# Second scan of a two-layer SSM/MoE kernel: who empties the bank of a gate projection

## The reference

```python
proj = hidden_states @ in_proj_w.T
gate = proj[..., :D_IN]                       # D_IN = 512
xBC  = proj[..., D_IN:D_IN + CONV_DIM]        # CONV_DIM = 768
...
xBC = silu(conv_b + causal_conv(xBC, 4 taps))
y   = _ssd(x * dt[..., None], dt * A, Bm, Cm) + D * x
hg  = y * silu(gate)
y   = hg * rsqrt(mean(hg * hg) + EPS) * norm_w
return y @ out_proj_w.T
```

## Time and profile before

| what | us |
|---|---|
| median of 3 runs (lowest to highest) | 1231.43 (1230.41 to 1232.26) |
| the profiled execution | 1236.41 |
| its span, first to last instruction | 1234.7 |
| PE busy | 982.6 (80%) |
| DVE busy | 913.9 (74%) |
| ACT busy | 491.2 (40%) |
| POOL busy | 430.8 (35%) |

### The profile page before, as it was taken

One profiled execution on the slowest core, in us unless ns is written; L12 is line 12 of the kernel. 1 busy time (PEld: TensorE's weight loads), 2 busy tenths in 40 slices (PEclk: granted clock), 3 DMA queues, 4 the chain that ended last, 5 costly groups with the idle time before them and its releaser, 6 DMA issues.

```text
span 1234.7 us, 18601 instructions
## 1 busy us (share of the span) xinstructions
PE 982.6 (80%) x6048; PEld 581.1 (47%) x6048; DVE 913.9 (74%) x1506; ACT 491.2 (40%) x1114; POOL 430.8 (35%) x332
## 2 busy tenths in 40 slices
PE   3987997788877877774587768889887988789885
PEld 2354455454444444443434444546554554455553
DVE  4758667989999999987586654766677667766577
ACT  2200135455555555441230144544444444544442
POOL 0000101777778778741270012322223222223220
PEclk9989999998999999985888898989999998999898
DMA  7950252878878878879620133434333333334324
GB/s 223 375 144 1 94 116 86 153 138 168 151 143 169 152 146 160 151 123 238 103 73 1 26 82 82 108 82 95 84 92 83 84 83 83 92 83 106 88 41 139
DMA packets 107092, 143.27 MB, mean 116 GB/s; under 512 B 30022, under 2 KB 97334, under 8 KB 102710
## 3 DMA queue, kind: packets, MB, share of 16 engines
q0 software_dynamic: 30368, 77.92, 32.9%
q1 hardware_dynamic: 76630, 64.14, 19.0%
HBM read 72.80 MB, written 39.46 MB: 91 GB/s over the span
## 4 chain that ended last, share of the span: by engine, by line
PE 39%; DVE 20%; DMA 13%; issue 11%; POOL 9%; ACT 6%; SPq 1%; ACTq 0%; DVEq 0%; POOLq 0%
DMA sum<-yo,to_i 10%; PE bank L686 7%; PE bank L698 4%; PE bank L1846 4%; POOL sum L1164 4%; POOL xg L1171 3%; PE bank L1429 3%; PE bank L1436 3%; DVE cv L2100 3%; PE bank L1897 2%; POOL y L1156 2%; PE bank L1829 2%; PE bank L1838 1%; PE bank L1870 1%; DVE areaD L2045 1%
## 5 line engine op out<-in xcount | busy, mean ns | idle before, releaser
L1501 POOL DMA_INDIRECT sum<-yo,to_i x48 | 77.2, 1608 | 345.2 <-ACT yo L1456 340.3
L1164 POOL DMA_INDIRECT sum<-yo,to_i x80 | 140.3, 1753 | 47.3 <-DMA sum<-yo,to_i 23.7
L1171 POOL DMA_INDIRECT xg<-xn_d,token_i x80 | 94.3, 1178 | 175.3 <-DVE to_i L460 93.4
L1011 PE MATMUL bank<-areaA,xgT 128*128 x320 | 122.7, 509 | 15.3 <-issue 9.0
L1028 PE MATMUL bank<-areaA,hidT 88*128 x320 | 92.2, 411 | 45.7 <-ACT hidT L1076 41.9
L2045 DVE TENSOR_TENSOR areaD<-areaD,gb 128x512 f32<-128x512 f32 x128 | 87.5, 689 | 38.1 <-ACT areaD L1992 34.7
L1992 ACT ACTIVATE areaD<-bank 128x512 f32<-128x512 f32 x128 | 76.1, 594 | 43.0 <-PE bank L1838 41.8
L1028 PEld LDWEIGHTS bank<-areaA,hidT 88*128 88x128 f32 x320 | 55.9, 194 | 76.4 <-issue 71.8
L686 PE MATMUL bank<-xnT,areaB 128*128 128x512 f32 x192 | 86.8, 599 | 0.8 <-DVE y L716 0.8
L1011 PEld LDWEIGHTS bank<-areaA,xgT 128*128 128x128 f32 x320 | 57.6, 199 | 59.1 <-issue 43.4
L1846 PE MATMUL bank<-xnT,w_in 128*128 128x512 f32 x160 | 83.0, 644 | 2.0 <-ACT ecn L1751 1.5
(11 more groups left out here) (340 smaller groups left out, 2158.0 us busy)
## 6 DMA issues: line engine op xcount, KB each, us to landing
y<-xnT POOLq DMA_DIRECT2D x21, 1024.0 KB
wst<-gu_f SPq DMA_DIRECT2D x96, 176.0 KB
y<-areaB POOLq DMA_DIRECT2D x11, 1024.0 KB
wst<-down_f SPq DMA_DIRECT2D x48, 176.0 KB
areaA<-in_gu SPq DMA_DIRECT2D x2, 2816.0 KB
gu_f<-in_gu POOLq DMA_DIRECT2D x1, 5632.0 KB, 17.4
sum<-yo SPq DMA_DIRECT2D x2, 2176.0 KB, 16.2
down_f<-in_down POOLq DMA_DIRECT2D x1, 2816.0 KB, 23.2
```

The lines of the kernel that those rows point to most:

```text
L1011: last = nc.tensor.matmul(bank[:, GB + q % 2, 0:2 * FI], xgT[:, q % 2, k, :], wgu0_of(e, k), start=(k == 0), stop=(k == KD - 1))
L1164: nc.gpsimd.indirect_dma_start(sum0_d[q % 2], bass.IndirectOffsetOnAxis(ap=to_i[:, q:q + 1], axis=0), yo[:, q % 5, :], None, compute_op=AL ...
L1171: nc.gpsimd.indirect_dma_start(xg[:, q % 5, :], None, xn_d[0], bass.IndirectOffsetOnAxis(ap=token_i[:, q:q + 1], axis=0)).then_inc(s.gathe ...
L1501: nc.gpsimd.indirect_dma_start(sum1_d, bass.IndirectOffsetOnAxis(ap=to_i[:, q:q + 1], axis=0), yo[:, q % 4, :], None, compute_op=ALU.add). ...
```

## The change

ACT, after the tanh, copies the gate projection itself into its place in gz (a second pass over the bank) and frees the bank with that. DVE multiplies in place: it reads tanh from tb and z from gz, both in SBUF, and writes gz. It no longer frees the bank, but waits until the bank is free, that is, until the copy is done. The semaphore gate_th, by which DVE waited for the tanh, is gone; a new one, gate_done, counts DVE's gates, and ACT waits on it before it writes a half of tb again (for g = 2 and 3, where it waited for the bank of the projection two before). For batches 2 and 3 ACT also waits until hg of two batches before is complete (hg_ready), since gz is shared with it.

```diff
@@ -1322,7 +1322,7 @@
-        conv_sum, conv_tanh, conv_out, gate_th = (sem(n) for n in ("conv_sum", "conv_tanh", "conv_out", "gate_th"))
+        conv_sum, conv_tanh, conv_out, gate_done = (sem(n) for n in ("conv_sum", "conv_tanh", "conv_out", "gate_done"))
@@ -1964,8 +1964,11 @@
                     if g < 2:
                         act.wait_ge(conv_out, b * 6 + 5 + g)
                     else:
-                        taken(act, b, "proj", m - 2)
-                    nc.scalar.activation(tb[:, g % 2, :], o, ACT.Tanh, scale=0.5).then_inc(gate_th, 1)
+                        act.wait_ge(gate_done, b * G1 + g - 1)
+                    if b > 1:
+                        act.wait_ge(hg_ready, (b - 1) * PAIRS)
+                    nc.scalar.activation(tb[:, g % 2, :], o, ACT.Tanh, scale=0.5)
+                    nc.scalar.activation(gz[b % 2][:, g, :], o, ACT.Copy).then_inc(free, 1)
@@ -2105,9 +2108,9 @@
             def gate_silu(b, g):
 
-                o, free = take(v, b, "proj", 6 + g)
-                v.wait_ge(gate_th, b * G1 + g + 1)
-                nc.vector.scalar_tensor_tensor(gz[b % 2][:, g, :], tb[:, g % 2, :], 1.0, o, ALU.add, ALU.mult).then_inc(free, 1)
+                taken(v, b, "proj", 6 + g)
+                z = gz[b % 2][:, g, :]
+                nc.vector.scalar_tensor_tensor(z, tb[:, g % 2, :], 1.0, z, ALU.add, ALU.mult).then_inc(gate_done, 1)
```

## The result

The changed kernel takes 1230.11 us in the median of 20 runs (1218.43 to 1238.36), where the kernel before, run beside it, takes 1232.57 (1225.91 to 1243.16, 20 runs). The ratio is 0.9954, with a 95% interval from 0.9933 to 0.9975: 5.7 us faster, and not less than 3.1 nor more than 8.3 (each times 1232.57). It is faster by more than the 0.2%, and the forecast of 1229.1 us within 1223.5 to 1234.5 holds; but of the 5.7 us it foretold less than half, 2.35. The two medians lie only 2.5 us apart, close to the forecast; the ratio is nearer to that of the means (1228.4 and 1234.0 us, with the changed kernel's one slow run, 1238.36, left out), and I go by it.

A forecast was written before the change was run, and what follows sets the result against it. PE was taken as the fullest engine, with hand-overs between engines filling most of the chain. Gains of 6.3 us less 3.0 and 0.95 gave 2.35 us, so 1231.43 became 1229.1 us, range 1223.5 to 1234.5.

The forecast's parts named there:

- the six gates of the gains: m = 6 of batches 1 to 3, m = 9 of batches 2 and 3, m = 8 of batch 3: 6.3 us gained.
- Rival A: The copies are hidden in the loop; all 9.1 us come, less the prologue: 8.15 us gained, 1223.3 us; chance 0.15.
- B: Costs arrive, gains don't, since DVE is the next bound: 3.95 us lost, 1235.4 us; chance 0.17.
- C: PE's waits in the loop pass to other conditions and the costs are absorbed: 0 us, 1231.4 us; chance 0.13.
- D: Prologue idle time shifts the granted clock; two more projections at the low level cost 3.6 us, 1232.7 us; chance 0.05.
- The freed bank: In the loop, PE's eight waits for the gate instruction go: 6.3 of 9.1 us gained, nothing at m = 7.
- The copies in the loop: At six of twelve loop gates the copy delays an awaited hidT or exp by 0.5 us: 3.0 us lost.
- The prologue: For batch 0, the first gate comes 0.45 us later and the third 0.5 more: 0.95 us lost.

The follow-up runs named there:

- copy_late: The change with ScalarE's loop copy put behind the expert's part that follows the tanh; ratio to the kernel before 0.9944.
- copy_only: The kernel before with the 16 copies added on ScalarE, the bank still freed by VectorE; ratio to before 1.0061, median 1242.64 us.
- six_gates: The kernel before with the change at only the six gates where a gain was forecast; ratio to before 0.9918, median 1225.01 us.
- ten_gates: The kernel before with the change at only the other ten gates, prologue included; ratio to before 1.0035, median 1236.97 us.
- gate_first: The kernel before, without copies, VectorE's twelve loop gates moved to the head of their group; ratio to before 0.9897, run again 0.9924.
- gate_later: The change with VectorE's gates one group later, behind the products of the group after; ratio to the kernel before 0.9931.
- first_copied: The change with VectorE's gates at the head of their group, as in gate_first; ratio to the kernel before 0.9894, median 1215.9 us.

## Why the prediction was right, and where its sizes were off

**The mechanism held.** All eight waits for the gate went. At m = 7 of batches 1 and 3 they gave nothing. The copies cost up to their 0.5 us where hidT or the exp was awaited, and nothing at the six gates of the gains. One reading was incomplete: behind m = 8 of batch 2 I had only hidT delayed, but copy_late shows that with hidT on time the exp alone costs the same 0.5 us. Rival A was refuted by copy_only, B by six_gates. C doesn't fit a ratio whose interval ends at 0.9975, nor the six pieces that got shorter. D can't be seen in pieces chosen for their full clock; the ratio came out alike twice, 0.9954 and 0.9951, but part of it is the clock's, as shown below.

**Three terms were mis-sized; together they made the gain too small.**
- *The freed bank.* At m = 6 I had the three waits give their idle times, 0.58, 1.15 and 0.99 us. They gave 0.15 us more each: 0.73, 1.30 and 1.15. At m = 9 of batch 2 it was 1.51 for 1.3, at m = 9 of batch 3 1.35 for 1.4, and at m = 8 of batch 3 0.63 for 0.9; PE there stops 0.73 us for the sum of squares. In all 6.7 us for my 6.3. That m = 9 of batch 3 came out right was luck: in this trace PE stood 0.71 us ahead of the down product, where before it stood 0.47. In the second trace of the change it stood 0.47 again, and the two m = 9 gave 1.59 and 1.79 us, which makes 7.2 in all.
- *The copies in the loop* cost 0.32, -0.03 and 0.43 us in batch 1 (the first from ten_gates, as the change's own piece was at the low clock), and 0.49 three times: 2.2 us for my 3.0. The -0.03 behind m = 8 of batch 1 isn't a copy without cost. PE's wait for hidT grew from 0.16 to 0.64 us there, while the 0.45 us that it had waited for the crow rows' DMA is absent in the changed trace. Between kernels that both have this DMA wait the copy costs 0.48 us (ten_gates 12.19, before 11.71), between kernels without it 0.32 (the change 11.68, six_gates 11.36). Why the DMA is sometimes in time isn't shown.
- *The prologue:* in the five traces without copies in it PE's wait for the hidden values ends 29.46 to 29.48 us behind the first projection of batch 0, in the seven with them at 29.84 to 29.93: 0.4 us for my 0.45. (The length of the wait, 2.70 us before and 3.11 after, also depends on the clock ahead of it; without copies it is anything from 2.70 to 3.34.) Up to batch 1's first projection it is 43.71 us for 43.07, 0.6 us for my 0.95.

Together 6.7 - 2.2 - 0.6 = 3.9 us by the pieces, where I had 2.35, and where the times say 5.7 with an interval that begins at 3.1. The prologue of the changed kernel on the timeline, against the earlier trace rows:

```profile
741.34 0.69 DVE L2113 SCALAR_TENSOR_TENSOR areaD<-tb,areaD 128x512 f32<-128x512 f32 x1 [0.28 <-ACT areaD L1971]
...
742.71 0.42 PE L1423 MATMUL bank<-ident,hid 128*88 128x128 f32 x2 [3.11 <-DVE hid L1470]
```

**The clock, which the sum left out.** The 2 us between 3.9 and 5.7 are within the interval, but copy_only, ten_gates, six_gates and gate_first's first series also came out farther from before than their pieces, by some 1 to 4 us. The mean granted clock of each execution tells how much of it ran at 1.2 GHz: the share is twice what the mean lacks to 1. Among the executions of one kernel, each us more at 1.2 GHz goes with 0.28 to 0.37 us more of time (a straight line through them, for each kernel with ten executions or more). At 0.35 this gives an estimate. copy_only had on average 9.9 us more at 1.2 GHz than before, which is 3.4 of its 7.7 us (by means); ten_gates 8.5 us more, 3.0 of its 4.9. The change, in its second series, had 3.5 us less, 1.2 of its 5.6, and the 4.4 that are left fit the pieces. gate_first had 12.4 us less, 4.3 of its 11.8, and 7.5 are left: less than its pieces' 9.4, but still 3 more than for the change. Only six_gates isn't helped: it had no less than before. So much of what the pieces don't show goes with the clock. Whether these kernels cause the difference or chance does isn't settled; for gate_first it came out alike on both chips (12.4 and 11.7 us less). One sign of rival D is in the prologue: the second stretch at 1.2 GHz there was twice as long in three of the seven traces with copies in it (copy_only, gate_later, first_copied), and batch 1's first projection came 44.9 to 45.2 us behind batch 0's, where in the other four it was 43.4 to 43.7. In none of the five without copies was it so. Twelve traces are too few to be sure.

**On the Trainium skill.** The 62 cycles by which the Trainium skill (VectorE: DVE Perf Modes, section on the TRN2 errata) has a source in SBUF cheaper than one in PSUM don't show here: 683 ns from the bank, 683 to 688 from SBUF. Its rule (the same page, Rules for kernel authors), to copy first only for many operations, looks at the operation itself. For that it was right: copy_only is 7.5 us slower. As a forecast of the change, rival B, it failed, since the copy also bought an early bank; but gate_first gets that by a reordering, without the copy.

## What to carry to other kernels

If TensorE waits for a bank, ask first whether the engine that empties it was idle before it did so. Moving that instruction ahead in its queue adds no work (here it delayed something at two of twelve gates, by 0.27 and 0.12 us against the copy), while a copy on another engine is paid wherever somebody waits for that engine next. An engine that is half idle on the page can still be the one awaited at a given place: look at what stands right behind the new instruction, and whether a short wait for it (here 0.16 us) is already there. And compare kernels by pieces between the same instructions at the same granted clock; here most repeat to 0.02 us while whole executions of one kernel scatter by 5 to 25.

## What the runs showed of the hardware

An idle time of PE in front of a matmul is not its whole price. In the trace of before, gb's first matmul started 1.15 us after the end of the one ahead; without the wait it starts 0.14 us before that end, as the rows of m = 6 above show (946.95, while L1830 runs from 946.81 for 0.28 us). So the wait cost 1.30 us, and at all three m = 6 gates the piece shrank by 0.15 to 0.16 more than the idle time shown; in the second trace of the change the two m = 9 shrank by 0.17 more (1.79 for 1.62, 1.59 for 1.42). The ends of matmuls are modelled in the profile, but the pieces run from start to start and don't depend on them. It is so only where nothing else stops PE: behind m = 8 of batch 3 a wait of 1.42 us gave 0.63.
